# Experts computed on routed tokens only, through slots in device memory, and attention as one stream over batches and groups

## The reference

```python
# attention: 16 heads of size 8, 8 batches of 512 tokens
q = xn @ wq;  lat = xn @ w_down;  k = lat @ wk_up;  v = lat @ wv_up
q, k = rope(q), rope(k)
scores = q k^T / sqrt(8), masked so that page(key) <= page(query), pages of 32 tokens
s = softmax(scores) @ v, heads joined, @ wo
# experts: 8 experts, hidden size 256, two per token
logits = silu(xn @ rw1 + rb1) @ rw2 + rb2
w = softmax over the two largest logits, 0 elsewhere
y = xn + sum_e w_e * (silu(xn @ ew1[e] + eb1[e]) @ ew2[e] + eb2[e])
out = x + s * silu(y)
```

## Time and profile before

| | us |
|---|---|
| median of 3 runs | 667.03 (665.81 to 667.17) |
| span of the profiled execution, first to last instruction | 663.7 |
| median less span | 3.4 |
| PE busy (4116 matmul instructions) | 607.3, 92% |
| PE weight loads, beside the matmuls | 448.6, 68% |
| DVE busy (1199) | 467.0, 70% |
| ACT busy (507) | 354.4, 53% |
| POOL busy (20) | 18.6, 3% |
| mean granted clock of TensorE, share of full speed | 0.971 |

### The profile page before, as it was taken

The page is one execution under the profiler, slowest core; times in us unless marked ns, Lnnn a source line. Parts: engine busy times, 40 slices in busy tenths (PEclk is TensorE's granted clock), DMA queues, the critical chain, the costliest instruction groups (busy, mean ns, idle before and its releaser), DMA issues.

```text
span 663.7 us, 12438 instructions
## 1 busy us (share of the span) xinstructions
PE 607.3 (92%) x4116; PEld 448.6 (68%) x4116; DVE 467.0 (70%) x1199; ACT 354.4 (53%) x507; POOL 18.6 (3%) x20
## 2 busy tenths in 40 slices
PE   2569999999999999999999999999999999999895
PEld 1448855787567865678557875788656885578643
DVE  6677866787568866798667865698757875687502
ACT  2123456643766347754576438653576445763573
POOL 0000000000000100001000000001000000000000
PEclk9758999999999989999999999999999998999999
DMA  5810002100120002200021001200021001200000
GB/s 170 210 43 2 3 13 61 27 1 19 38 60 1 18 1 49 46 1 18 21 51 25 1 18 45 50 1 18 1 67 28 2 17 25 51 22 2 19 1 16
DMA packets 21798, 20.93 MB, mean 32 GB/s; under 512 B 4545, under 2 KB 14450, under 8 KB 21778
## 3 DMA queue, kind: packets, MB, share of 16 engines
q1 hardware_dynamic: 21778, 20.67, 12.9%
HBM read 5.45 MB, written 2.10 MB: 11 GB/s over the span
## 4 chain that ended last, share of the span: by engine, by line
PE 70%; DVE 13%; issue 12%; ACT 2%; SPq 1%; DMA 1%; DVEq 0%; POOLq 0%; POOL 0%; ACTq 0%
PE bank L500 15%; PE bank L580 10%; PE ring L517 7%; PE ring L562 7%; PE bank L446 5%; PE bank L447 5%; PE bank L448 5%; PE bank L517 5%; DVE row_max L861 5%; PE ring L565 2%; DVE acc L908 2%; PE ring L566 2%; PE bank L462 1%; ACT probs L683 1%; PE bank L478 1%
## 5 line engine op out<-in xcount | busy, mean ns | idle before, releaser
L683 ACT ACTIVATE probs<-ring 128x768 f32<-128x768 f32 (+1 forms) x192 | 158.9, 880 | 79.7 <-PE ring L562 48.8
L861 DVE TENSOR_REDUCE row_max<-ring 128x2 f32<-128x256 f32 (+1 forms) x192 | 152.3, 819 | 13.1 <-PE ring L517 13.0
L643 ACT ACTIVATE eh<-bank,bias_cols 128x512 f32<-128x512 f32 x128 | 87.8, 686 | 136.9 <-PE bank L448 134.9
L500 PE MATMUL bank<-ew_sb,eh 128*128 128x128 f32 x1024 | 125.8, 276 | 2.4 <-DVE x_lo L786 2.4
L500 PEld LDWEIGHTS bank<-ew_sb,eh 128*128 128x128 f32 x1024 | 120.1, 192 | 5.6 <-issue 3.8
L517 PE MATMUL ring<-k_head,q_stack 108*128 108x256 f32 (+2 forms) x384 | 93.4, 344 | 12.3 <-DVE row_max L861 11.2
L517 PEld LDWEIGHTS ring<-k_head,q_stack 108*128 108x128 f32 x384 | 66.7, 194 | 37.0 <-DVE row_max L861 24.8
L580 PE MATMUL bank<-probs,v_cols 128*32 128x512 f32 (+3 forms) x1024 | 88.0, 442 | 0.4 <-ACT probs L683 0.4
L908 DVE SCALAR_TENSOR_TENSOR acc<-bank,gate_w,acc 128x128 f32<-128x128 f32 x224 | 63.1, 345 | 32.3 <-PE bank L500 32.1
L856 DVE TENSOR_REDUCE row_max<-bank 128x1 f32<-128x128 f32 (+3 forms) x128 | 58.9, 487 | 32.6 <-PE bank L517 31.7
L562 PE MATMUL ring<-q_stack,k_head 128*128 128x512 f32 (+1 forms) x256 | 71.8, 395 | 3.5 <-ACT probs L683 3.5
(11 more groups left out here) (115 smaller groups left out, 659.4 us busy)
## 6 DMA issues: line engine op xcount, KB each, us to landing
k_stack<-roped_hi SPq DMA_DIRECT2D x64, 64.0 KB, 2.0
q_stack<-roped_hi SPq DMA_DIRECT2D x64, 64.0 KB, 2.0
k_stack<-roped_lo SPq DMA_DIRECT2D x32, 64.0 KB, 2.0
q_stack<-roped_lo SPq DMA_DIRECT2D x32, 64.0 KB, 2.0
out<-out_sb SPq DMA_DIRECT2D x8, 256.0 KB, 2.3
x_all<-in_L_attn_x SPq DMA_DIRECT2D x4, 448.0 KB, 6.9
probs<-in_L_ffn_ew SPq DMA_DIRECT2D x1, 1024.0 KB, 5.8
q_stack<-neg_rows SPq DMA_DIRECT2D x32, 16.0 KB
```

What stands on the lines that cost most here:

```text
L500: last = mm(ps[:, t * E:(t + 1) * E], eh[:, s % EH_RING, t * P:(t + 1) * P], ew2_sb[:, e, f, :], start=(f == 0), stop=(f == HALVES - 1))
L643: nc.scalar.activation(eh[:, s % EH_RING, :], wide[s % 2][:], ACT.Silu, bias=bias_cols[:, s:s + 1]).then_inc(hidden_done, 1)
L683: nc.scalar.activation(probs[:, n % 2, r:r + 2, lo:T], ring[:, r:r + 2, lo:T], ACT.Exp, scale=SCALE).then_inc(exp_done, 1)
L861: V.tensor_reduce(row_max[:, g, i, 2 * pair:2 * pair + 2], ring[:, 2 * (m % 2):2 * (m % 2) + 2, 0:(i + 1) * P], AX, ALU.max).then_inc(max_ ...
```

## The change

What it does, part by part (names as in the new kernel):

- The steps are one list without loops, `program()`: an opening, then 32 windows (8 batches x 4 groups), then an end. A window has three steps of scores (two halves each), and between them the maxima of the next window and the first two of the one after, and `fills` (projections, rope, split, stacks, heads, outputs).
- PSUM has one ring of 6 banks, `ring`, for all jobs in the order of the program (`placement()`); scores, maxima, projections, output rows and expert jobs take two adjacent banks, the others one. A job waits for the readers of what lay in its banks. `wide` (2 banks) is left for pv.
- The opening normalizes all batches (batch 0 on DVE, the others on ACT), and makes x columns, router and logits of all 8 batches. x columns are made a second time for the projections.
- Projections, router and experts are plain float32 products and no longer three float32r ones.
- Routing is done once, on all 4096 tokens, in windows 0 and 1: top two, a running count of tokens per expert (a product with a triangular matrix for the partition part), the place of each pair in a table of 39 tiles x 256 slots, and the expert of each tile. Experts start at tile boundaries.
- The table `slot_rows` lies in device memory. It is zeroed by DMA in the opening; 64 indirect DMAs from POOL scatter the rows of xn. `w_pack`, also in device memory, has per expert the weights of both layers and both biases.
- 10 bursts of 4 tiles (the last of 3) stand at the end of windows 9 to 18. SP loads each tile's expert weights (by a register read from `tile_e`) and slot rows; PE transposes the slots, ACT loads the table of silu, PE and ACT make layer 1, PE layer 2, DVE adds the bias, and SP stores the rows in `y_rows`.
- 64 indirect DMAs from POOL gather each token's two rows; DVE adds them, weighted, to xn (`combine`, windows 23 to 30).
- The attention output of a batch is stored in device memory (`s_rows`) and fetched in the end, with x, when the places of the weights and slots are free; gates (silu) and results are computed in the last windows and the end.

The diff rewrites most of the file. Its core, as lines of the new kernel:

```diff
+NBANK = 6
+ROWS = 256
+NTILE = (2 * B * T + NE * (ROWS - 1)) // ROWS
+BURST = 4
+DVE_GROUPS = (0, 1)
...
+def window(b, g, route):
+
+    w = NG * b + g
+    nb, ng = (w + 1) // NG, (w + 1) % NG
+    ahead = [maximum(w + 1, 2) + maximum(w + 1, 3), maximum(w + 1, 4) + maximum(w + 1, 5),
+             maximum(w + 2, 0) + maximum(w + 2, 1)]
+    burst = w - FIRST_BURST
+    run = 0 <= burst < NBURST
+    seq = []
+    if burst == -1:
+        seq += [("load", i, k) for i in (0, 1) for k in tiles_of(i)]
+    if GATHER_FROM <= w < GATHER_FROM + B:
+        seq.append(("gather", w - GATHER_FROM, 0))
+    for k, fill in enumerate(fills(b, g)):
+        n = 3 * g + k
+        if k == 2 and run:
+            seq.append(("slots_in", burst, 0))
+        seq += [("scores", b, 2 * n)] + ahead[k][0:1] + [("scores", b, 2 * n + 1)] + ahead[k][1:2]
+        if n >= 1:
+            seq.append(("pv", b, n - 1))
+        elif b >= 1:
+            seq.append(("pv", b - 1, NSTEP - 1))
+        if k == 1 and nb < B:
+            seq.append(("negate", nb, ng))
+        seq += fill
+        for _ in range(4):
+            if route:
+                seq.append(route.pop(0))
+        if k == 1 and nb < B:
+            seq.append(("neg_max", nb, ng))
+    if run:
+        seq += [("silu_table", burst, 0), ("layer1", burst, 0), ("layer1", burst, 1), ("layer2", burst, 0),
+                ("layer2", burst, 1), ("exp_table", burst + 1, 0), ("store_rows", burst, 0)]
+        if burst + 2 < NBURST:
+            seq += [("load", burst + 2, k) for k in tiles_of(burst + 2)]
+    if 0 <= w - COMBINE_FROM < B:
+        seq.append(("combine", w - COMBINE_FROM, 0))
+    if b == B - 1 and g >= 2:
+        seq += [("fetch", c, 0) for c in range(3 * g - 6, 3 * g - 3)]
+    return seq
...
-            def split_product(ps, w_hi, w_lo, b):
-
-                mm(ps, w_hi, x_hi[:], start=True, stop=False)
-                mm(ps, w_lo, x_hi[:], start=False, stop=False)
-                return mm(ps, w_hi, x_lo[:], start=False, stop=True)
...
+        def take(pe, step):
+
+            for prev in FREED[step]:
+                pe.wait_ge(done_of[prev[0]], COUNT[prev])
+            return ring[:, PLACE[step], :]
...
+            def load(burst, k):
+
+                if k == 0:
+                    sp.wait_ge(s_pack, 16 * 6)
+                    sp.wait_ge(tiles_ready, 1)
+                    sp.wait_ge(scattered, 16 * 2 * BT)
+                if burst >= 2:
+                    sp.wait_ge(y_ready, 2 * burst - 2)
+                expert = sp.value_load(tile_e[0:1, k:k + 1], min_val=0, max_val=NE - 1)
+                sp.dma_start(w_ring[:, k % W_RING, :],
+                             w_pack[bass.ds(expert, 1)].rearrange("o p w -> (o p) w")).then_inc(w_in_ring[k % W_RING], 16)
+                sp.dma_start(slots[:, k % W_RING, :, :], slot_rows[ROWS * k:ROWS * k + ROWS, :].rearrange(
+                    "(a p) d -> p a d", p=P)).then_inc(w_in_ring[k % W_RING], 16)
...
+            def layer1(burst, q):
+                if q == 0:
+                    pe.wait_ge(slots_ready, burst + 1)
+                ps = take(pe, ("layer1", burst, q))
+                for c in halves_of(burst, q):
+                    for f in range(HALVES):
+                        last = mm(ps[:, c % 2, f * ROWS:(f + 1) * ROWS], w_ring[:, BURST * (burst % 2) + c, f * P:(f + 1) * P],
+                                  slots_t[:, c * ROWS:(c + 1) * ROWS], start=True, stop=True)
+                last.then_inc(slot_full, 1)
+
+            def layer2(burst, q):
+                pe.wait_ge(hidden_ready, 2 * burst + q + 1)
+                ps = take(pe, ("layer2", burst, q))
+                for c in halves_of(burst, q):
+                    for a in range(2):
+                        for f in range(HALVES):
+                            last = mm(ps[:, c % 2, a * E:(a + 1) * E], hidden[:, c, f, a * P:(a + 1) * P],
+                                      w_ring[:, BURST * (burst % 2) + c, HID + f * E:HID + (f + 1) * E], start=(f == 0), stop=(f == HALVES - 1))
+                last.then_inc(slot_full, 1)
...
+            def scatter(b, n):
+
+                pool.wait_ge(place_ready, 1)
+                pool.wait_ge(zeroed, 16 * -(-(NTILE * ROWS // P * E) // ZERO))
+                pool.wait_ge(xn_ready, B)
+                for t in range(BT):
+                    for which in range(2):
+                        G.indirect_dma_start(slot_rows, bass.IndirectOffsetOnAxis(ap=place[:, which, t:t + 1], axis=0),
+                                             xn[:, t, :], None).then_inc(scattered, 16)
...
+            def combine(b, n):
+
+                dve.wait_ge(pairs_in[b % 2], 16 * 2 * TT * (b // 2 + 1))
+                if b == 0:
+                    dve.wait_ge(weights_ready, 1)
+                for which in range(2):
+                    for t in range(TT):
+                        at = TT * b + t
+                        ins = stt(out=xn[:, at, :], in0=pair_in[:, b % 2, which, t * E:(t + 1) * E],
+                                  scalar=pair_w[:, which, at:at + 1], in1=xn[:, at, :], op0=ALU.mult, op1=ALU.add)
+                    if which == 0:
+                        link(ins)
+                ins.then_inc(mixed, 1)
```

More of the change, by code:

```diff
@@ new lines, with counts, placement @@
+STEPS = program()
+BANKS = {"x_cols": 1, "proj": 2, "values": 1, "router": 1, "logits": 1, "max": 2, "scores": 2, "neg_max": 1, "out_rows": 2,
+         "out_cols": 1, "project": 1, "ranks": 2, "slots_in": 2, "layer1": 2, "layer2": 2}
+JOBS = [s for s in STEPS if s[0] in BANKS]
+JOB_AT = {s: j for j, s in enumerate(JOBS)}
+def counts():
+    seen, count = {}, {}
+    for s in STEPS:
+        assert s not in count, s
+        seen[s[0]] = count[s] = seen.get(s[0], 0) + 1
+    return count
+def placement():
+    at, holder, place, freed = 0, [None] * NBANK, {}, {}
+    for s in JOBS:
+        n = BANKS[s[0]]
+        at = (at + at % n) % NBANK
+        place[s] = slice(at, at + n)
+        freed[s] = sorted({h for h in holder[at:at + n] if h}, key=JOB_AT.get)
+        holder[at:at + n] = [s] * n
+        at = (at + n) % NBANK
+    return place, freed
@@ L952, in _ @@
+            run({"prep": prep, "consts": consts, "stats": row_stats, "norm": norm, "proj": proj, "split": split, "heads": heads,
+                 "max": max_scores, "negate": negate, "pv": pv, "values": values, "out_rows": out_rows, "logits": logits,
+                 "top": top_two, "gap": gap, "count": count, "ranks": ranks, "places": places, "weights": weights,
+                 "layer2": layer2, "combine": combine, "result": result})
         @block.gpsimd
```

1184 lines of the change are left out of this document (576 added, 608 removed).

## The result

The changed kernel takes **753.4 us** (median of 4 runs, 752.1 to 754.9), the kernel before 667.1 beside it: ratio 1.130 [1.128, 1.133]. Forecast were 585 us and "faster", with a range up to 655. Direction and size are both wrong. In the experiments all runs of a kernel lie within 1.5% of its fastest but two of the four of paced3, and those two are left out of its time.

A forecast was written before the change was run, and what follows sets the result against it. PE's instruction stream was taken to bound the kernel, with DVE level after the change. Opening 68 + windows 390 + routing 6 + scatter wait 3 + bursts 80 + combining 16 + end 19 = 582, plus 3.4: 585 us, range 508 to 655.

The forecast's parts named there:

- The gathers, 8 x 1.15 = 9 us a batch, fit in a window: Combine windows: a batch's eight indirect DMAs at 1.15 us each were to hide within one window.
- It just fits: Scatter: ends 96 us after the first exponential, SP waits for it at 100; about 3 us lost behind that wait.
- Rival B: Scatter decides and makes the kernel slower than before: 650 us at 2 us per indirect DMA, 780 at 3; chance 0.09.
- rival D: Stream windows looser, 14 us, or an opening of 85 us: 640 us in all; chance 0.18.
- Rival C: PE's clock falls in windows where it idles: 9.8 us becomes about 18, ten such windows cost 80, total 665; chance 0.05.
- PE was forecast busy 390 to 440: Whole kernel: TensorE's busy time expected near 390 to 440 us, against 607.3 before.
- Opening: Start to first exponential: normalization, router and logits of all 8 batches, 68 us, bounds 55 and 85.
- Routing: Windows 0 and 1: top two, counts and ranks done once on DVE, about 6 us; places ready 22 us after first exponential.
- Bursts: Ten windows ending with four expert tiles: 8 us extra each, 80 us in all, bounds 5 and 11 each.
- The other 20 windows: Stream windows at 12.2 us each, plus 3 us lost at the scatter wait and 16 us for combining.
- End: After the last exponential: a store and a fetch through device memory replace an add, 19 us against 12 before.
- 540 to 610: Whole kernel: the main forecast's range of time in us, given chance 0.50.

The follow-up runs named there:

- paced3: Changed kernel with the scatter's and gathers' indirect DMAs issued in groups of up to three per step of the stream: 684.1 us, 1.03 times the kernel before.
- no_indirect: Changed kernel without its 128 indirect DMAs (slots and gathered rows are zeros, output misses the experts' part): 638.96 us, ratio to before 0.961.
- The probes: Three single runs of the changed kernel without scatter and gathers, with trains of GpSimd operations added in windows 2, 5, 19 and 21; one took 636.9 us.
- gap9: Changed kernel with POOL clearing 512 columns of an unused buffer after each indirect DMA and waiting for it: 669.8 us, ratio to before 1.004.
- probe_c: no_indirect plus 16 scatters and 16 gathers, each awaiting the previous landing, 16 scatters with 0.54 us memsets between, and four gathers back to back: 636.9 us.
- s11_open: Complete kernel with indirect DMAs spread evenly, first burst in window 11, and opening's weight-packing and zero-writing DMAs issued by POOL, not ACT: 663.2 us, against 660.6 without that edit.
- probe_b: no_indirect plus trains: 16 scatters of 32 rows, 16 of 128 with memsets between, 8 gathers of 128, 16 of 64; window 2 took 26.1 us.

## Why the prediction was wrong

**The step that failed** is "The gathers, 8 x 1.15 = 9 us a batch, fit in a window", and "It just fits" for the scatter: 128 indirect DMAs entered the sum at 3 us, as work of an engine that nothing else needs. Their own size was right: POOL takes 0.97 and 0.96 us each and issues one per 1.27 (forecast 1.15, expected between 1.0 and 1.3). What was missed is what they do to others: issued back to back for 80 us, they hold up TensorE's completions, and its waiters idle up to 40 us at a time. no_indirect prices that at 114 us where 3 stood. The probes tie it to the indirect DMA and its density, and gap9 gets 84 of them back by nothing but memsets between them. I had bounded the DMA's own duration from both sides, and never what runs beside it: an idle engine hides only its own time.

**Rival B** ended on the right side for the wrong reason. It asked whether the scatter is done when SP needs it, and decided from 2.15 us each; at 1.27 that price is 64 x 0.07 = 4 us. (Its own formula gives 585 + 61 + 24 = 670 at 2.15, not the "about 665" beside it; and rival D's 585 + 58 is 643.) The mechanism is real, gap9 shows it with 19.3 us on SP, but only at a spacing of 1.8 and a later start than forecast. The Trainium skill (DMA: Bandwidth & Descriptors, Anatomy of one DMA) fits about 2.0 us plus the bytes for one DMA of GpSimd, an estimated 2.15 here; probe_c, where each waits for the one before, shows 2.5 (137.56 - 135.07), and the measurement decides; the changed kernel doesn't wait. The Trainium skill's other rule on that page, that DVE in its two-port modes locks GpSimd out of the state in which it writes descriptors (SWDGE vs HWDGE vs iDMA), has no sign here: POOL kept its 1.27 us through all 64 (1.53 at most). The harm ran the other way.

**Rival C**, the clock: the granted clock is 0.50, the lower of its two levels, in 140 to 200 us, after PE had come to a stop at 130, and 0.84 as a mean over the run (0.92 in no_indirect). But it follows the stalls: in window 2 no_indirect reads 1.00 where the changed kernel reads 0.50 (in window 1 both read 0.67 and 0.66). So it explains no more than the step from 507 to 530 in PE's busy time. PE was forecast busy 390 to 440, so its work was priced at least 15% too low with no such stall in it; 0.92 as the mean clock is part of that, and how large a part is open.

**The other terms**, by the profile of no_indirect, where the spans add up to 632.3 us: 80.4 to the first exponential, 532.2 to the end of the last, 19.8 behind it.
- Opening: 68 forecast, 80.4 measured (81.1 in the changed kernel). The steps in the changed kernel's timeline: the power on POOL took 4.81 us for 28 elements a partition ("1 to 3"), the 28 normalizations 10.88, to 50.1 instead of 41; the seven rounds 24 us as forecast 22. I first blamed the nine DMA issues on ACT's queue (13.7 to 38.6); s11_open refutes it.
- Routing: "about 6 us in windows 0 and 1". To the end of window 1 it took 127.5 - 80.4 = 47.1 us, where 2 x 12.2 + 6 = 30.4 stood: 17 more. The likely reason is that DVE's short steps hang on one another, with the stream's reductions between them; no run varied that. The places came 35 us after the first exponential, not 22.
- Bursts: windows 9 to 18 took 441.2 - 225.1 = 216.1 us, 21.6 each, where 12.2 + 8 stood: 14 more.
- The other 20 windows took 269, where 20 x 12.2 + 3 + 16 = 263 stood: right as an average, though it is made of first windows of 18.4 to 20.1, others of 12 to 14, and three short ones at the end (11.3, 9.4, 5.2).
- End: 19 forecast, 19.8.

Together 12 + 17 + 14 + 6 + 1 = 50 = 632.3 - 582; with 119 for the indirect DMAs (751.6 - 632.3, by the profiled runs; 114 by the medians), the changed kernel's 751.6. Without the step that failed the answer would have been 639, 4% faster: right in sign and inside the range, and outside "540 to 610" all the same. Four of these five terms were too low by 6 us or more and none too high. (The 3.4 us added for the difference of time and span were 1.9.)

## What to carry to other kernels

An idle engine isn't a free one: before you put a long train of instructions of a new kind on it, price what the train does to the others, and where no row shows it, measure a train of 16 beside the running stream first. Indirect DMAs are to be spread: some 2 in 4 us (64 in 119 us) cost some 5 us over this kernel, 64 in a row stop it. Memsets between them also help, but they lengthen VectorE's work. And where work of a serial chain (routing, statistics) enters a packed stream, count its links, not its busy time.

## What the runs showed of the hardware

- A train of indirect DMAs 1.27 us apart delays what waits for TensorE: idle times of up to 40 us in the changed kernel, 9 to 13 us lost by a train of 16. A train of 8 cost some 5 us (windows 24 to 30 of the changed kernel: 30.7 us for six; window 19 of probe_b: 17.6 against 11.9), one of four nothing (window 19 of probe_c: 12.0). Scatter or gather, 32 or 128 rows make no difference; 16 plain DMAs of POOL at 544 ns cost 1.3 us at most.
- At 1.8 us apart a train of 16 left no late completion, and at 2.5 nothing that shows at all. The windows with memsets in the gaps lost 3.3 us at 1.8 apart and 4.9 at 2.2; 0.9 and 3.9 of that are VectorE's own work grown longer, and the rest is within the spread of single windows (2.5).
- Memsets on POOL lengthen some of VectorE's instructions: four k_head pieces from 1.9 to 4.9 us beside a train of memsets of 1024 columns, all 64 from 27.2 to 34.3 us in gap9; its reductions keep their 6.3 us a window.
- Waiters on DVE's and ACT's signals saw no such delay. Why TensorE alone, and whether its work or its signal is late, stays open; that the waiters go on one each 4.9 to 5.8 us, in the order of PE's products, points to the signals.
- A power of 128x28 elements on POOL takes 4.81 us, one of 128x4 1.02: more elements cost more, though not in proportion.
